# Message loop of a graph kernel: the index tiles of the gathers are filled by transfers of the sync engine in place of GpSimd copies

## The chip, the cores and the metric

One core of a Trainium2 chip runs the whole kernel in one launch. The metric is the device time of that core in microseconds, median over the runs. Engines are PE (TensorE), DVE (VectorE), ACT (ScalarE), POOL (GpSimd) and SP (SyncE). In this kernel SP only issues DMAs, and POOL issues the gathers.

## What is computed

The reference puts four graph layers behind one another on 625 nodes of 512 values: a mean aggregation, a transformer over the edges, a weighted graph convolution, and a message layer over 20,000 edges. The change is in the last:

```python
def _L3_gnn_ref(x, edge_index, edge_attr, W1, b1, W2, b2, W3, b3, W4, b4, gamma, beta):
    src, dst = (edge_index[0], edge_index[1])
    edge_feat = jnp.concatenate([x[src], x[dst], edge_attr], axis=-1)
    h = mish(edge_feat @ W1 + b1)
    messages = mish(h @ W2 + b2)
    agg = jax.ops.segment_sum(messages, dst, num_segments=x.shape[0])
    u = mish(jnp.concatenate([x, agg], axis=-1) @ W3 + b3)
    out = u @ W4 + b4
    y = x + out
    ...
```

## The kernel before

`edge_layer` is the last of the kernel's stages and takes its second part, from about 877 us on. x @ W1 is not computed per edge: two tables, src_table and dst_table, hold x times the two blocks of W1 for each node, and an edge needs one row of each, added. The edges are sorted by target. A tile is 128 edges, a pair is 2 tiles (PT = 2), a group is 2 pairs, so 512 edges; there are 40 groups (PAIRS = 80 pairs, the last group nearly empty). The loop goes pair by pair: one step per pair, and `run_steps` writes it on every engine, 16 steps ahead of a hardware loop of 4 steps a pass and some steps behind it. `s(n)` and `g(n)` give the step and the group with a lag, `on(n)` says whether the step of n before exists, and `a` is the step modulo 4.

What each engine does in a step:

- POOL: waits until the ring buffer is free (semaphore turned: PE has transposed the pair that was four before, so a count of s-3), and issues two gathers of the first table for pair s (L1661, into ring buffer a of 4). Then it waits for the landing of those of the pair before and issues two gathers of the second table for pair s-1, which add onto the first (L1692). In every even step, from 12 on, it also issues an addition of a finished group's sums to agg in HBM (L1706).
- PE: transposes the gathered rows of a pair (L1762), adds the attributes' product (L1770, L1771), sums an older pair by its one-hot tile (L1795), and multiplies by W2 in three parts, 24 matmuls (L222).
- ACT and DVE: the two Mish functions, each a chain that goes between them. The first: ACT L1887, DVE L1977, ACT L1893, L1895, L1897, DVE L2020, then DVE splits the result in two parts (L2029, L2031) for PE. The second: DVE L2003, ACT L1903, DVE L2023, ACT L1906, L1909, L1890, DVE L1984. In even steps DVE also makes the one-hot tile (L1994), takes the sums (L2017) and splits the attributes (L2040, L2042).
- SP: loads the attributes of a group (L1621) into one of two slots when the split of the group before in that slot is done (attr_low).

The row numbers that a gather reads lie in an index tile: `index[0]` and `index[1]`, each of 128 x 2 x 2 x 2 int32 (4 KB), hold the numbers of one group, source and target. All numbers lie in SBUF in `pair_index` from the start of the stage on. In an even step, POOL waits for turned, then for the landing of the second-table gathers of pair s-3, which are the last readers of the tile (dst_added), and then copies 128 x 8 numbers out of `pair_index` (`copy_index`, L1655). It waits for its own copy (index_ready, L1656) and goes on with the gathers. `settle` is an increment of a semaphore that nobody waits for; the waits ahead of it in POOL's sequencer are carried by it (L163 in the profile).

Of the kernel before, what the change touches and what calls it, by code (L numbers as in the profile page):

```python
# [159 lines left out]
def settle(k, eng):  # L160


    eng.sem_inc(k.settled, 1)  # L163
# [1302 lines left out]
def edge_layer(nc, k):  # L1466

    PT = 2
    EDGE = PT * P
    RING = 4  # L1470
    LATE = 4
    OWN = [(m, f) for m in range(KF) for f in range(2)]
    ctx = ExitStack()
    with ctx:
        sb, pb, sem = scope(ctx, nc, "edge")
# [7 lines left out]
        pair_index = sb("pair_index", [P, TILES // PT, 2, PT], I32)  # L1483
        index = [sb(f"index{a}", [P, 2, 2, PT], I32) for a in range(2)]
# [28 lines left out]
        ps_sum = [pb(f"sump{a}", [P, D]) for a in range(2)]  # L1513
        S = {n: sem(n) for n in (
            "loaded_once", "index_made", "vec", "sca", "made", "w1_split", "zeroed", "var_ready", "rstd_ready", "h_ready",
            "index_ready", "turned", "z1_made", "attr_high", "attr_low",
            "e1_ready", "u1_ready", "inner1_ready", "q1_ready", "h1_ready", "hi_ready", "lo_ready",
            "z2_made", "z2_ready", "e2_ready", "u2_ready", "square2_ready", "log2_ready", "q2_ready", "h2_ready",
            "onehot_ready", "pair_summed", "sum_taken", "mish_vec", "mish_sca", "u_ready",
# [5 lines left out]
        from_loaded = [sem(f"from_loaded{a}") for a in range(RING)]  # L1525
        dst_added = [sem(f"dst_added{a}") for a in range(RING)]
        attr_loaded = [sem(f"attr_loaded{a}") for a in range(2)]
        PAIRS = GROUPS * TPG // PT
        DEPTH = 16
        low, high = slice(0, EATTR), slice(EATTR, P)  # L1530
# [49 lines left out]
        with nc.Block() as block:  # L1580
            @block.sync
            def _(sp):
                sp.dma_start(b1[:, :], k.dram["b1"][None, :].to_broadcast([P, D])).then_inc(loaded["b1"], 16)
                for part in (low, high):
                    sp.dma_start(w1_raw[part, :], k.dram["w1"][2 * D:2 * D + EATTR, :]).then_inc(S["loaded_once"], 16)
                sp.dma_start(w2, k.dram["w2"].rearrange("(c p) n -> p c n", p=P)).then_inc(loaded["w2"], 16)
                sp.dma_start(b2, k.dram["b2"][None, :].to_broadcast([P, D])).then_inc(S["loaded_once"], 16)
                halves = k.dram["w3"].rearrange("(c p) n -> p c n", p=P)
                sp.dma_start(w3[0], halves[:, 0:KF, :]).then_inc(loaded["w3"], 16)
                sp.dma_start(b3[:, :], k.dram["b3_cols"]).then_inc(loaded["b3"], 16)  # L1590
                rows_used = LAST_EDGES // TPG
                for n, name in enumerate(("src_tiles", "dst_mark")):
                    for t in range(TPG):
                        tile = (GROUPS - 1) * TPG + t
                        sp.dma_start(last_raw[t * rows_used:(t + 1) * rows_used, n:n + 1],
                                     k.dram[name][0:rows_used, tile:tile + 1],
                                     allow_slow_non_contiguous=True).then_inc(S["last_loaded"], 16)
                sp.wait_ge(S["zeroed"], 1)
                for i in range(NT):
                    sp.dma_start(k.agg[i * P:(i + 1) * P, :], zero).then_inc(zero_stored, 16)  # L1600
                sp.dma_start(k.agg[NP:NP + WIN, :], zero[0:WIN]).then_inc(zero_stored, 16)
                for name, table, stored in (("src", k.src_table, src_stored), ("dst", k.dst_table, dst_stored)):
                    for i in range(NT):
                        tab.need(sp, (name, i))
                        sp.dma_start(table[i * P:(i + 1) * P, :], tables[name][:, i, :]).then_inc(stored, 16)

                last_attr = k.dram["attr_T"][:, (GROUPS - 1) * GROUP:GROUPS * GROUP].rearrange(
                    "f (t p) -> f t p", t=TPG)[:, :, 0:LAST_EDGES // TPG]

                def step(s, g, a, on, is_late):  # L1610
                    if a % 2 == 0 and on(0):

                        slot, o = a // 2, g(0) % GROUPS
                        if on(4):

                            sp.wait_ge(S["attr_low"], g(2))
                        for part in (low, high):
                            if is_late and is_late(0) == LATE:
                                sp.dma_start(attr[slot][part, 0:LAST_EDGES], last_attr).then_inc(attr_loaded[slot], 16)
                            else:  # L1620
                                sp.dma_start(attr[slot][part, :], k.dram["attr_T"][:, bass.ds(o * GROUP, GROUP)]  # L1621
                                             ).then_inc(attr_loaded[slot], 16)

                n = run_steps(sp, step)

                for name in ("b4", "gamma", "beta"):
                    sp.dma_start(rows[name], k.dram[name][None, :].to_broadcast([P, D])).then_inc(loaded["rows"], 16)
                tab.need(sp, ("own",) + OWN[-1])
                sp.dma_start(w3[1], halves[:, KF:2 * KF, :]).then_inc(loaded["w3b_w4"], 16)
                sp.dma_start(w4, k.dram["w4"].rearrange("(c p) n -> p c n", p=P)).then_inc(loaded["w3b_w4"], 16)  # L1630

                sp.wait_ge(sum_stored, (n * GROUPS + (GROUPS - LATE)) * 16)

                sp.wait_ge(S["turned"], n * PAIRS + (PAIRS - 1))
                for i in range(NT):
                    sp.dma_start(agg[:, i, :].bitcast(F32), k.agg[i * P:(i + 1) * P, :]).then_inc(agg_loaded[i], 16)
                for i in range(NT):
                    sp.wait_ge(S["x_ready"], i + 1)
                    sp.dma_start(k.dram["out"][i * P:(i + 1) * P, :], k.x[:, i, :]).then_inc(out_stored, 16)
                sp.wait_ge(out_stored, 16 * NT)  # L1640

            @block.gpsimd
            def _(pool):
# [1 line left out]
                pool.wait_ge(S["made"], 1)  # L1645
                pool.memset(attr_w_rest[high, :].bitcast(F32), 0.0).then_inc(S["made"], 1)
                pool.wait_ge(S["made"], 2)
                pool.wait_ge(S["index_made"], 2)

                def copy_index(s, g, a, last=False):  # L1650
                    if last:
                        pool.wait_ge(S["last_ready"], 2)
                    settle(k, pool)
                    pair = last_index[:, :, :, :] if last else pair_index[:, bass.ds(s(0) % PAIRS, 2), :, :]
                    pool.tensor_copy(index[a // 2][:, :, :, :], pair).then_inc(S["index_ready"], 1)  # L1655
                    pool.wait_ge(S["index_ready"], g(-2))  # L1656
                    settle(k, pool)

                def gather_src(a):
                    for j in range(PT):  # L1660
# [2 lines left out]
                            in_offset=bass.IndirectOffsetOnAxis(ap=index[a // 2][:, a % 2, 0, j:j + 1], axis=0)  # L1663
                        ).then_inc(from_loaded[a], 16)

                for a in (0, 2):
                    copy_index(lambda add: a + add, lambda lag: (a - lag) // 2, a)
                pool.wait_ge(src_stored, 16 * NT)
                settle(k, pool)
                for a in range(RING):  # L1670
# [5 lines left out]
                def step(s, g, a, on, is_late):  # L1676
                    if on(0) and on(4):

                        pool.wait_ge(S["turned"], s(-3))
                        settle(k, pool)  # L1680
                        if a % 2 == 0:

                            pool.wait_ge(dst_added[(a - 3) % RING], s(-3) // RING * (16 * PT) + 16 * PT)
                            copy_index(s, g, a, is_late and is_late(0) == LATE)
                        gather_src(a)
                    if on(1):

                        ring = (a - 1) % RING
                        pool.wait_ge(from_loaded[ring], s(-1) // RING * (16 * PT) + 16 * PT)
                        settle(k, pool)  # L1690
                        for j in range(PT):
                            pool.indirect_dma_start(  # L1692
                                out=from_rows[ring][:, j, :].bitcast(F32), out_offset=None, in_=k.dst_table,
                                in_offset=bass.IndirectOffsetOnAxis(ap=index[ring // 2][:, ring % 2, 1, j:j + 1], axis=0),
                                compute_op=ALU.add).then_inc(dst_added[ring], 16)

                    if a % 2 == 0 and on(14) and not (is_late and is_late(14)):

                        pool.wait_ge(sum_stored, g(14) * 16 + 16)
                    if a % 2 == 0 and on(12) and not (is_late and is_late(12)):  # L1700

                        slot = a // 2
                        start = pool.value_load(k.starts[0:1, bass.ds(g(12), 1)], min_val=0, max_val=NP)
                        pool.wait_ge(S["sum_taken"], g(10))
                        settle(k, pool)
                        pool.dma_start(k.agg[bass.ds(start, WIN), :].rearrange("n (s c) -> s n c", s=2),  # L1706
                                       sum_rows[slot][:, :], accum_op=ALU.add).then_inc(sum_stored, 16)
# [511 lines left out]
```

## Time and profile before

| | |
|---|---|
| median of 3 runs | 1679.72 us (1679.65 to 1692.11) |
| the profiled execution's own time | 1672.88 us |
| its span in the profile | 1671.0 us, mean granted clock 0.987 |
| busy share of the span | PE 94%, DVE 71%, ACT 66%, POOL 41% |
| steady part of the message loop | about 1000 to 1560 us, 17.15 us a group |
| additions to agg issued by POOL | 36 |

The profile is one execution. A timeline row gives the start, the duration, the engine, the line of the program, the operation and its tiles, the count of instructions merged into the row, and in brackets the idle time of the engine before it with what ended it. "issue" there means that the profile shows nothing it waited for. A row of a DMA on POOL shows the time in which POOL writes its descriptors, not the transfer. A row of POOL's sequencer has the engine name POOLq, one of SP's SPq. Spans on POOL are rough.

### The profile page before, as it was taken

What the parts mean: (1) busy time and instruction counts of PE and PEld (TensorE: products, weight loads), DVE (VectorE), ACT (ScalarE), POOL (GpSimd) and SP (SyncE); (2) the same over time, 40 slices, a digit from 0 to 9 for tenths busy, and PEclk for the clock granted to TensorE, in tenths of its full rate; (3) what the DMA queues carried; (4) which work ended last, traced back from release to release, by engine and by line L of the source; (5) the groups of instructions that cost most, each with busy time, mean ns of one, the idle gap of its engine ahead of it and who ended that gap; (6) DMA issues with size and microseconds to landing.
All of it is one profiled execution on the core that took longest, in us unless ns stands there. A gap on an engine that the chain in (4) does not pass through costs nothing. (4 is left out here: it accounts for less than half of the span.)

```text
span 1671.0 us, 25082 instructions
## 1 busy us (share of the span) xinstructions
PE 1566.8 (94%) x8530; PEld 1218.3 (73%) x8530; DVE 1190.2 (71%) x1900; ACT 1097.2 (66%) x1531; POOL 686.0 (41%) x495
## 2 busy tenths in 40 slices
PE   5789699999999999999999999999999999999987
PEld 4765486878687868877854777777777777777774
DVE  8867546564655546565733588989989898998967
ACT  9841536554554455444530699999999999999962
POOL 3410120110012001200302788888888888888500
PEclk9999799999999999999999999999999999999989
DMA  3001140013002200211107767677777777777710
GB/s 104 0 19 65 39 133 25 1 51 113 26 20 67 85 21 32 62 52 63 53 1 228 156 139 150 145 144 148 138 152 144 148 145 142 151 135 155 162 38 31
DMA packets 107046, 153.94 MB, mean 92 GB/s; under 512 B 42042, under 2 KB 47034, under 8 KB 106466
## 3 DMA queue, kind: packets, MB, share of 16 engines
q0 software_dynamic: 72832, 87.84, 27.3%
q1 hardware_dynamic: 34146, 65.21, 12.0%
q8 instruction: 41, 0.67, 0.2%
q14 instruction: 27, 0.22, 0.0%
HBM read 141.02 MB, written 11.73 MB: 91 GB/s over the span
## 5 line engine op out<-in xcount | busy, mean ns | idle before, releaser
L1692 POOL DMA_INDIRECT edge_gathered<-dst_table,edge_index x158 | 257.3, 1629 | 57.4 <-issue 53.9
L222 PE MATMUL edge_z2p<-edge_w_hi,edge_h_hi 128*128 128x512 f32 x628 | 255.3, 407 | 6.8 <-issue 3.5
L1661 POOL DMA_INDIRECT edge_gathered<-src_table,edge_index x158 | 221.5, 1402 | 85.3 <-issue 33.6
L222 PE MATMUL edge_z2p<-edge_w_hi,edge_h_lo 128*128 128x512 f32 x628 | 248.5, 396 | 0.0
L222 PE MATMUL edge_z2p<-edge_w_lo,edge_h_hi 128*128 128x512 f32 x628 | 248.3, 395 | 0.0
L904 POOL TENSOR_TENSOR tr_cw<-w_c,tr_cw 32x1024 fp32r<-32x1024 f32 x8 | 19.0, 2373 | 367.5 <-ACT tr_cw L1118 367.5
L915 POOL TENSOR_TENSOR h<-h,tr_row_b 128x512 f32<-128x512 f32 x40 | 61.1, 1562 | 263.9 <-ACT C L1160 263.6
L222 PEld LDWEIGHTS edge_z2p<-edge_w_hi,edge_h_hi 128*128 128x128 f32 x628 | 117.9, 188 | 61.3 <-issue 36.3
L2020 DVE SCALAR_TENSOR_TENSOR edge_early<-edge_early,edge_z1p 128x1024 f32<-128x1024 f32 x79 | 96.5, 1221 | 59.8 <-ACT edge_early L1897 44.0
L222 PEld LDWEIGHTS edge_z2p<-edge_w_hi,edge_h_lo 128*128 128x128 f32 x628 | 118.0, 188 | 28.5
L222 PEld LDWEIGHTS edge_z2p<-edge_w_lo,edge_h_hi 128*128 128x128 f32 x628 | 118.1, 188 | 24.9
L931 PE MATMUL tr_one<-tr_yT_hi,tr_w_hi 128*128 128x256 f32 (+1 forms) x384 | 118.5, 309 | 5.0 <-issue 4.4
L931 PE MATMUL tr_one<-tr_yT_hi,tr_w_lo 128*128 128x256 f32 (+1 forms) x384 | 117.5, 306 | 0.0
L931 PE MATMUL tr_one<-tr_yT_lo,tr_w_hi 128*128 128x256 f32 (+1 forms) x384 | 117.5, 306 | 0.0
L1893 ACT ACTIVATE edge_early<-edge_early 128x1024 f32<-128x1024 f32 x79 | 83.5, 1056 | 48.8 <-DVE edge_early L1977 46.4
L1017 PE MATMUL tr_two<-tr_kT,tr_qT 128*128 128x320 f32 x320 | 101.7, 444 | 1.4 <-ACT C L1211 1.3
L1205 ACT ACTIVATE hT<-hT,tr_nmax 128x640 f32<-128x640 f32 x56 | 46.3, 827 | 83.7 <-DVE tr_nmax L1368 82.5
L2003 DVE TENSOR_TENSOR edge_late<-edge_z2p,w_c 128x1024 f32<-128x1024 f32 x79 | 96.5, 1222 | 4.9 <-PE edge_z2p L222 1.1
L2031 DVE TENSOR_TENSOR edge_h_lo<-edge_early,edge_h_hi 128x1024 fp32r<-128x1024 f32 x79 | 96.9, 1226 | 2.7
L1984 DVE SCALAR_TENSOR_TENSOR edge_late<-edge_late 128x1024 f32<-128x1024 f32 x79 | 95.8, 1213 | 0.3 <-ACT edge_late L1906 0.3
L1895 ACT ACTIVATE edge_early<-edge_early 128x1024 f32<-128x1024 f32 x79 | 83.7, 1060 | 2.5
L1897 ACT ACTIVATE edge_early<-edge_early 128x1024 f32<-128x1024 f32 x79 | 83.6, 1058 | 2.5
(356 smaller groups left out, 3985.8 us busy)
## 6 DMA issues: line engine op xcount, KB each, us to landing
w_c<-in_attr_T SPq DMA_DIRECT2D x78, 128.0 KB
agg<-edge_sum_rows POOLq DMA_DIRECT2D x36, 128.0 KB
w_a<-in_wv SPq DMA_DIRECT2D x4, 1024.0 KB, 5.3
w_b<-in_wq SPq DMA_DIRECT2D x4, 1024.0 KB, 5.4
w_a<-in_wk SPq DMA_DIRECT2D x4, 1024.0 KB, 7.7
w_b<-in_wo SPq DMA_DIRECT2D x4, 1024.0 KB, 7.0
w_a<-in_m SPq DMA_DIRECT2D x4, 1024.0 KB, 5.4
w_b<-in_m SPq DMA_DIRECT2D x4, 1024.0 KB, 5.3
```

What stands on the lines that cost most here:

```text
L222: mm = pe.matmul(out, a, b, start=(n == 0), stop=(n == last))
L931: mm = pe.matmul(out, a, b, start=(start and n == 0), stop=(stop and n == len(terms) - 1))
L1017: mm = pe.matmul(bank[:, f, 0:HALF], qT[:, h, i * P:(i + 1) * P], kT[:, h, f * HALF:(f + 1) * HALF], start=True, stop=True)
L1661: pool.indirect_dma_start(out=from_rows[a][:, j, :].bitcast(F32), out_offset=None, in_=k.src_table, in_offset=bass.IndirectOffsetOnAxis(ap ...
L1692: pool.indirect_dma_start(out=from_rows[ring][:, j, :].bitcast(F32), out_offset=None, in_=k.dst_table, in_offset=bass.IndirectOffsetOnAxis ...
L1893: act.activation(m1[one], m1[one], ACT.Square).then_inc(S["inner1_ready"], 1)
L1895: act.activation(m1[one], m1[one], ACT.Ln, bias=1.0).then_inc(S["inner1_ready"], 1)
L1897: act.activation(m1[one], m1[one], ACT.Exp, scale=-1.0).then_inc(S["q1_ready"], 1)
L1984: dve.scalar_tensor_tensor(h2[new], m2[new], 0.5, z2[new], ALU.subtract, ALU.mult).then_inc(S["h2_ready"], 1)
L2003: dve.tensor_tensor(cols(z2[two], D), cols(ps_z2[:, :], D), b2[:, None, :].to_broadcast([P, PT, D]), ALU.add).then_inc(S["z2_ready"], 1)
L2020: dve.scalar_tensor_tensor(m1[one], m1[one], 0.5, ps_z1[one][:, :], ALU.subtract, ALU.mult).then_inc(S["h1_ready"], 1)
L2031: dve.tensor_tensor(h1_lo[one][:, :, :], cols(m1[one], EDGE), h1_hi[one][:, :, :].bitcast(F32), ALU.subtract).then_inc(S["lo_ready"], 1)
```

## The change

The copy on POOL goes. SP fills the index tiles by a DMA from `pair_index` to `index[slot]`, both in SBUF. POOL signals that a tile is free (index_free) at the end of the odd step before the one that needs it, after it has waited there for the landing of the second-table gathers of pair s-2 (which is pair s-3 as seen from the even step). In the even step POOL waits for the DMA's landing (index_loaded) instead of copying. In SP's order the wait for index_free and the new DMA stand ahead of the attribute loads of the same step; the first two fills stand ahead of the table stores. The last group's tile comes from `last_index`, by the same DMA.

```diff
+        index_loaded = [sem(f"index_loaded{a}") for a in range(2)]
...
                 sp.dma_start(k.agg[NP:NP + WIN, :], zero[0:WIN]).then_inc(zero_stored, 16)
+                sp.wait_ge(S["index_made"], 2)
+                for slot in range(2):
+                    sp.dma_start(index[slot][:, :, :, :], pair_index[:, 2 * slot:2 * slot + 2, :, :]).then_inc(index_loaded[slot], 16)
...
                         if on(4):
-
+                            at = s(0) % PAIRS
+
+                            sp.wait_ge(S["index_free"], g(2))
+                            if is_late and is_late(0) == LATE:
+                                sp.wait_ge(S["last_ready"], 2)
+                                pair = last_index[:, :, :, :].rearrange("p a b c -> p (a b c)")
+                            else:
+                                pair = pair_index[:, :, :, :].rearrange("p a b c -> p (a b c)")[:, bass.ds(at * (2 * PT), 4 * PT)]
+                            sp.dma_start(index[slot][:, :, :, :].rearrange("p a b c -> p (a b c)"), pair).then_inc(index_loaded[slot], 16)
                             sp.wait_ge(S["attr_low"], g(2))
...
-                pool.wait_ge(S["index_made"], 2)
-
-                def copy_index(s, g, a, last=False):
-                    if last:
-                        pool.wait_ge(S["last_ready"], 2)
-                    settle(k, pool)
-                    pair = last_index[:, :, :, :] if last else pair_index[:, bass.ds(s(0) % PAIRS, 2), :, :]
-                    pool.tensor_copy(index[a // 2][:, :, :, :], pair).then_inc(S["index_ready"], 1)
-                    pool.wait_ge(S["index_ready"], g(-2))
-                    settle(k, pool)
...
-                for a in (0, 2):
-                    copy_index(lambda add: a + add, lambda lag: (a - lag) // 2, a)
+                for slot in range(2):
+                    pool.wait_ge(index_loaded[slot], 16)
...
                         if a % 2 == 0:
-
-                            pool.wait_ge(dst_added[(a - 3) % RING], s(-3) // RING * (16 * PT) + 16 * PT)
-                            copy_index(s, g, a, is_late and is_late(0) == LATE)
+                            pool.wait_ge(index_loaded[a // 2], g(0) // 2 * 16 + 16)
+                            settle(k, pool)
                         gather_src(a)
...
+                    if a % 2 == 1 and on(-1) and on(3):
+
+                        pool.wait_ge(dst_added[(a - 2) % RING], s(-2) // RING * (16 * PT) + 16 * PT)
+                        pool.sem_inc(S["index_free"], 1)
```

How it moves instructions on POOL, in the hardware loop, from the odd step to the even step behind it. Before (edge_index is the index tile, edge_gathered the ring, ISA and REGISTER_ALU are the sequencer's):

```order
L1661 DMA edge_gathered<-src_table,edge_index 128x512 [waits edge_turned]
L1661 DMA edge_gathered<-src_table,edge_index 128x512
L1689 ISA
L1692 DMA edge_gathered<-dst_table,edge_index 128x512 [waits edge_from_loaded0]
L1692 DMA edge_gathered<-dst_table,edge_index 128x512
L1655 ISA [waits edge_turned,edge_dst_added3]
L1655 COPY edge_index<-edge_pair_index 128x8
L1656 REGISTER_ALU
L1661 DMA edge_gathered<-src_table,edge_index 128x512 [waits edge_index_ready]
```

The same place after the change:

```order
L1663 DMA edge_gathered<-src_table,edge_index 128x512 [waits edge_turned]
L1663 DMA edge_gathered<-src_table,edge_index 128x512
L1690 ISA
L1693 DMA edge_gathered<-dst_table,edge_index 128x512 [waits edge_from_loaded0]
L1693 DMA edge_gathered<-dst_table,edge_index 128x512
L1684 ISA [waits edge_dst_added3,edge_turned]
L1663 DMA edge_gathered<-src_table,edge_index 128x512 [waits edge_index_loaded1]
```

The copy and the wait for it are gone, and the wait for the landing (dst_added) now stands ahead of the one for turned, with the increment of index_free between them, which is no row here. SP's queue in the hardware loop before, two steps:

```order
L1621 ISA [waits edge_attr_low]
L1621 DMA w_c<-in_attr_T 64x512 x2
L1621 ISA [waits edge_attr_low]
L1621 DMA w_c<-in_attr_T 64x512 x2
L1569 ISA
```

and after the change:

```order
L1627 ISA [waits edge_index_free]
L1627 DMA edge_index<-edge_pair_index 128x8
L1633 ISA [waits edge_attr_low]
L1633 DMA w_c<-in_attr_T 64x512 x2
L1627 ISA [waits edge_index_free]
L1627 DMA edge_index<-edge_pair_index 128x8
L1633 ISA [waits edge_attr_low]
L1633 DMA w_c<-in_attr_T 64x512 x2
```

Each pair of attribute loads now has the index transfer and its wait ahead of it. PE, ACT and DVE keep their order.

## Rows read from the trace of the kernel before

**Rows 1.** Waits, message loop (920 to 1630): who waited for whom: us, times, longest.
```profile
ACT edge_early L1893 <- DVE edge_early L1977: 46.4, 39, 3.1
DVE edge_early L2020 <- ACT edge_early L1897: 44.0, 52, 3.3
...
POOL edge_gathered L1661 <- POOL edge_index L1655: 30.6, 38, 0.8
...
PE edge_z1p L1762 <- DMA edge_gathered<-dst_table,edge_index: 1.6, 1, 1.6
```

**Rows 2.** Timeline of ACT, one group: start, duration, instruction, idle before.
```profile
1313.15 1.06 ACT L1893 ACTIVATE edge_early<-edge_early 128x1024 f32<-128x1024 f32 x1 [1.14 <-DVE edge_early L1977]
...
1323.28 1.06 ACT L1897 ACTIVATE edge_early<-edge_early 128x1024 f32<-128x1024 f32 x1
...
1330.32 1.06 ACT L1893 ACTIVATE edge_early<-edge_early 128x1024 f32<-128x1024 f32 x1 [1.17 <-DVE edge_early L1977]
```

**Rows 3.** Timeline of DVE, the same group.
```profile
1317.57 0.69 DVE L2023 TENSOR_SCALAR edge_late<-edge_late 128x1024 f32<-128x1024 f32 x1
...
1324.37 1.22 DVE L2020 SCALAR_TENSOR_TENSOR edge_early<-edge_early,edge_z1p 128x1024 f32<-128x1024 f32 x1 [0.45 <-issue]
...
1326.11 0.70 DVE L2029 CAST edge_h_hi<-edge_early 128x1024 fp32r<-128x1024 f32 x1
...
1327.99 0.65 DVE L2040 CAST edge_attr_parts<-w_c 128x512 fp32r<-128x512 f32 x1
...
1329.45 0.84 DVE L1977 TENSOR_SCALAR edge_early<-edge_early 128x1024 f32<-128x1024 f32 x1
```

**Rows 4.** Timeline of PE, transposes of three pairs in the same group.
```profile
1312.73 0.81 PE L1762 MATMUL edge_z1p<-edge_ident_r,edge_gathered 128*128 128x128 f32 x8
...
1321.39 0.80 PE L1762 MATMUL edge_z1p<-edge_ident_r,edge_gathered 128*128 128x128 f32 x8
...
1329.86 0.80 PE L1762 MATMUL edge_z1p<-edge_ident_r,edge_gathered 128*128 128x128 f32 x8
```

**Rows 5.** Line L163 on POOL's sequencer, 1313.4 to 1313.8: ns, first and last start.
```profile
L163 POOLq EVENT_SEMAPHORE  x2: 17/17/17, 1313.6 to 1313.7; - x2
```

**Rows 6.** Timeline of POOL, the same group.
```profile
1316.17 1.56 POOL L1692 DMA_INDIRECT edge_gathered<-dst_table,edge_index  x1 [0.30 <-issue]
1317.16 1.12 POOL L1655 COPY edge_index<-edge_pair_index 128x8 int32 x1
1319.08 2.03 POOL L1661 DMA_INDIRECT edge_gathered<-src_table,edge_index  x1 [0.80 <-POOL edge_index L1655]
...
1325.14 1.75 POOL L1692 DMA_INDIRECT edge_gathered<-dst_table,edge_index  x1 [0.30 <-issue]
1326.31 2.08 POOL L1706 DMA_DIRECT2D agg<-edge_sum_rows  x1
1328.69 1.08 POOL L1661 DMA_INDIRECT edge_gathered<-src_table,edge_index  x1 [0.30 <-issue]
```

**Rows 7.** Timeline of POOL, start of the loop: last gather of pair 1, first copy.
```profile
923.59 1.53 POOL L1692 DMA_INDIRECT edge_gathered<-dst_table,edge_index  x1 [0.30 <-issue]
...
929.25 0.34 POOL L1655 COPY edge_index<-edge_pair_index 128x8 int32<-128x8 int32 x1 [0.46 <-DMA edge_gathered<-dst_table,edge_index]
```

**Rows 8.** SP: its waits from 880 to 1630, and its attribute issues near 1312.5 (ns).
```profile
SPq L1621 <- DVE edge_attr_parts L2042: 556.3, 37, 16.0
...
L1621 SPq DMA_DIRECT2D w_c<-in_attr_T x2: 475/648/822, 1312.5 to 1313.0; - x2
```

**Rows 9.** DMA issues from 920 to 1630: count, size, median us to landing.
```profile
edge_gathered<-agg SPq DMA_DIRECT2D x5, 256.0 KB, 4.1
```

**Rows 10.** Timeline of DVE, before the first addition to agg.
```profile
985.42 0.42 DVE L2040 CAST edge_attr_parts<-w_c 128x512 fp32r<-128x512 f32 x1
...
986.59 0.69 DVE L1977 TENSOR_SCALAR edge_early<-edge_early 128x1024 f32<-128x1024 f32 x1
```

**Rows 11.** Timeline of DVE, end of the loop, beside an addition to agg.
```profile
1583.14 0.98 DVE L2029 CAST edge_h_hi<-edge_early 128x1024 fp32r<-128x1024 f32 x1
```

More of the change, by code:

```diff
@@ L1515, in edge_layer @@
             "loaded_once", "index_made", "vec", "sca", "made", "w1_split", "zeroed", "var_ready", "rstd_ready", "h_ready",
-            "index_ready", "turned", "z1_made", "attr_high", "attr_low",
+            "turned", "index_free", "z1_made", "attr_high", "attr_low",
             "e1_ready", "u1_ready", "inner1_ready", "q1_ready", "h1_ready", "hi_ready", "lo_ready",
```

## Prediction

> **What bounds the kernel now.** I read the waits of the message loop first, then a timeline of one group (two steps) on each engine, then the same instructions at another phase of the loop. The table of waits says who is late: ACT waits for DVE (46.4 us, 39 times), DVE for ACT (44.0 us, 52 times), and PE waited for a gather once in its loop stretch, 1.6 us [rows 1]. The longest wait that the change touches is POOL's own, 30.6 us in 38 waits for its copy [rows 1]: it belongs to an engine that nobody waits for.
>
> The timelines show why. From ACT's first instruction of a group, 1313.15, to its end at 1323.28 + 1.06 = 1324.34, ACT runs without a gap; at 1324.37 DVE's product L2020 starts, which waited for it, and DVE runs without a gap to the end of L1977, 1329.45 + 0.84 = 1330.29; at 1330.32 ACT's L1893 starts, which waited for that [rows 2, 3]. Start to start is 1330.32 - 1313.15 = 17.17 us: this ring of ACT and DVE is the group's period. PE is close behind: its transposes start at 1312.73, 1321.39 and 1329.86, so one step takes 8.66 us and the other 8.47 [rows 4]. The shorter is PE without a wait, so PE alone would need 2 x 8.47 = 16.94 us. The period can fall by 17.15 - 16.94 = about 0.2 us a group and no more, whatever happens on POOL.
>
> POOL looks full in its timeline, since every gather starts 0.3 us after the one before, but it has time to spare. The wait for the transposes that free the ring buffer (turned) is passed at 1313.6, in POOL's sequencer [rows 5], while the copy behind it runs only at 1317.16, after the two gathers already queued [rows 6]. That wait belongs to step s, and it asks for pair s-4, whose transposes ran at 1312.73. Pair s-3 is then transposed at 1321.39, s-2 at 1329.86, s-1 at 1338.5. The second-table gather of pair s-1 is issued until 1325.14 + 1.75 = 1326.89 [rows 6]. At the start of the loop a landing shows: issued until 923.59 + 1.53 = 925.12, landed when the copy was released at 929.25, 4.1 us later [rows 7]. So pair s-1 is there at 1331.0 and PE is 7.5 us from missing it.
>
> **The change, part by part.**
>
> *Removed: POOL's copy and its two waits.* The copy takes 1.12 us, of which 1317.73 - 1317.16 = 0.57 lie beside the gather before it (1316.17 + 1.56), and 0.80 of idle follows [rows 6]: 1.12 - 0.57 + 0.80 = 1.35 us a group, 1319.08 - 1317.73 as a check, and 40 groups make 54 us of POOL. Its cover is the 7.5 us of slack, so the end moves by 0. If the cover were gone these 54 us would be the gain, and nothing in the rows says it is.
>
> *Added on POOL:* the landing wait for pair s-3 moves from the start of the even step to the end of the odd one, with the increment of index_free; behind it in the queue stand only the wait for turned and the gathers of step s. It was passed at 1313.7 at the latest [rows 5], so POOL loses nothing by it.
>
> *Added on SP:* one issue a group, priced by its neighbours at 0.48 to 0.82 us [rows 8], and a wait in front of it that holds back the attribute loads of the same step. SP idles 556.3 us in 37 waits, 15 us a group [rows 8], and the split that reads them (L2040) comes for that slot two groups later, at 1327.99 + 17.15. Cost 0.
>
> *Added wait: index_loaded.* Signal at 1313.7, issue 0.5 to 0.8, landing between nothing and the 4.1 us of the nearest row, a 256 KB load [rows 9]: the tile is there between 1314.2 and 1318.6. POOL could start at 1317.73 + 0.30 = 1318.03. So the gathers of step s start at 1318.0 to 1318.9 in place of 1319.08; I take 1318.0, as 4 KB is the smaller end. POOL gains 1 us at first and up to 5 over the groups, until turned or the index stops it. All of it is slack.
> The Trainium skill (DMA: Bandwidth & Descriptors, Anatomy of one DMA) gives a fixed cost of some 2 us to a DMA from GpSimd, most of it completion; an estimate by it would put the tile at 1316.5, before POOL is free. It speaks against the exchange where the ring is short (the copy takes 0.34 us when POOL is idle [rows 7]); no run so far shows the cost for a small transfer of SP.
>
> *Start.* At step 4 POOL is not ahead: the copy starts at the landing, 929.25, takes 0.34, and the same 0.80 of idle follows: the gather comes 1.14 us later [rows 6, 7]. Now it is signal, issue and landing, 0.5 to 4.9 us: the gather comes between 0.6 us earlier and 3.8 us later, once. PE holds several ready pairs there. I take +1 us. The two first fills stand on SP before the table stores, which wait for DVE; 0.
>
> *Moved: POOL against DVE.* This is the term with a sign. In the ring of ACT and DVE stand two instructions that take longer than they need: L2040 0.65 and L1977 0.84 [rows 3]. Nineteen groups earlier, before the additions to agg began, they took 0.42 and 0.69 [rows 10]. The difference, 0.23 + 0.15 = 0.38 us, is in every group of the ring. Beside them POOL issues the addition to agg (ends 1326.31 + 2.08 = 1328.39) and a gather (ends 1328.69 + 1.08 = 1329.77) [rows 6]; L2040 ends 0.25 after the one and L1977 0.52 after the other, as if each had been let go then. With POOL 1 us or more earlier the addition ends near 1327.0 to 1327.4, before L2040 asks at 1327.99. Bounds: all 0.38 goes, but PE caps the gain at 0.2; or the same POOL work hits L2023 and L2029 of the ring. I take -0.1 us in the 33 to 36 groups with an addition: -3.5 us.
> The Trainium skill (SBUF — State Buffer, Who interferes with whom) states that DVE in its two-port mode and GpSimd share a port pair as an exclusive lock. The stretched rows agree with it. By it, taking any GpSimd copy away should also free DVE; the rows say that this copy stretches nothing: L2023 at 1317.57 takes 0.69 with the copy beside it at 1317.16, so that gain is 0.
>
> *Sum.* The profiled execution took 1672.88 us (span 1671.0): +1 - 3.5 = 1670.4. The median of the runs, 1679.72, is 6.84 above it; there the forecast is 1677.5.
>
> **Rivals.**
>
> *A, POOL's new place hits DVE harder (slower).* Mechanism: the addition and the gathers, now earlier, fall on L2023 and L2029, which stand in the ring (L2029 at 1326.11 with 0.70, L2023 right before it) [rows 3] and are not stretched today. Price: one such hit is shown at the end of the loop, L2029 0.98 us in place of 0.69, beside an addition [rows 11]. Two hits make +0.58 a group; if the 0.38 of today stays too, 36 x 0.58 = +21, 1700 us. It decides from 0.47 a group on (1% over 36 groups). Against it: POOL's addition already lies on L2029 today (from 1326.31) without stretching it.
>
> *B, the stretch goes altogether.* The ring falls to 17.15 - 0.38 = 16.8, PE holds at 16.94: 36 x 0.2 = -7, 1672.5 us. For it: a shift of 1 us suffices for L2040. Against: the gather behind the addition moves too and may stretch the next.
>
> *C, the new transfer is late.* PE waits once it lands more than 7.5 us after it should; each us beyond that costs up to 1 us a group, 2 us would be 1750. Nothing near it: 256 KB land in 4.1.
>
> *D, POOL doesn't come forward at all,* since the index lands at 1318.6 to 1319: nothing changes but the start, 1680.5.
>
> **How the numbers follow.** Forecast 0.50, A 0.14, B 0.20, C 0.03, D 0.13. The forecast's own range is 1672 to 1685. The runs of before differ among themselves by 0.4% (profiled against median) and more, so the low end is B less that, 1666; the high end takes in most of A, 1694. About 1% is what a measurement of this kernel can tell from no change, 16.8 us. Faster by that is closed by PE's 16.94 (0.2 x 36 = 7 us): 0.04, for an error in that floor. Slower by it are C and most of A: 0.14. Within: 0.82.
>
> **What would show it.** Right: POOL's waits for its copy are gone, POOL shows some idle time before the even step's gather or runs it near 1318.0 of the same phase, PE still waits for no gather, the group's period is 16.94 to 17.15, and L2040 falls towards 0.42. For A, L2023 or L2029 above 0.69 in most groups and a period above 17.5. For B, a period of 16.94 and PE without any wait for L2003. For C, PE waiting for second-table gathers in the loop. The prediction is wrong if the period moves by more than 0.2 downward, since then PE's floor was misread, or if ACT and DVE keep their ring and the time still rises.

## The result, and the profile after

The changed kernel takes 1716.36 us (median of 4 runs, 1710.29 to 1726.27), the kernel before 1680.4 beside it: ratio 1.020, 95% interval 1.0136 to 1.027. It is slower (the whole interval lies above 1; whether it is slower by 2% it leaves open), where I forecast 1677.5 and no change. The profiled execution took 1718.4 us, its span is 1716.5, which is 45.5 more than the 1671.0 of before.

The waits of the message loop after the change (920 to 1630; who waited for whom: us, times, longest):

```profile
POOL edge_gathered L1663 <- DMA edge_index<-edge_pair_index: 88.7, 33, 5.6
DVE edge_sum_rows L2022 <- DMA agg<-edge_sum_rows: 55.2, 27, 3.6
...
ACT edge_late L1914 <- DVE edge_late L2028: 45.0, 38, 3.2
DVE edge_early L2025 <- ACT edge_early L1902: 41.7, 43, 3.3
...
ACT edge_early L1898 <- DVE edge_early L1982: 32.7, 37, 3.1
...
PEld edge_z1p L1767 <- DMA edge_gathered<-dst_table,edge_index: 22.4, 19, 2.4
```

Against [rows 1] three waits are new or grown. POOL waits for the index transfer, 88.7 us in 33 groups, 2.7 each. DVE waits 27 times until an addition to agg has landed and the sums' buffer is free (55.2 us). PE's weight loads wait 19 times for gathered rows (22.4 us; PE itself waited once in the loop before). DVE and PE, which in the loop before waited for what POOL issues once at most, now do so in 19 and more groups: POOL has come onto the path.

POOL's timeline, one group after the change (start, duration, instruction, idle before; it answers [rows 6]):

```profile
1313.81 1.77 POOL L1663 DMA_INDIRECT edge_gathered<-src_table,edge_index  x1 [3.77 <-DMA edge_index<-edge_pair_index]
1315.89 1.45 POOL L1663 DMA_INDIRECT edge_gathered<-src_table,edge_index  x1 [0.30 <-issue]
1317.64 1.57 POOL L1693 DMA_INDIRECT edge_gathered<-dst_table,edge_index  x1 [0.30 <-issue]
1319.52 1.56 POOL L1693 DMA_INDIRECT edge_gathered<-dst_table,edge_index  x1 [0.30 <-issue]
1320.50 2.56 POOL L1711 DMA_DIRECT2D agg<-edge_sum_rows  x1
...
1328.81 1.56 POOL L1693 DMA_INDIRECT edge_gathered<-dst_table,edge_index  x1 [0.30 <-issue]
1332.44 1.19 POOL L1663 DMA_INDIRECT edge_gathered<-src_table,edge_index  x1 [2.07 <-DMA edge_index<-edge_pair_index]
```

SP's timeline in the same group, and below it pieces of the chain that ended last (start, duration, what), with the transfers of the group before and of the group after:

```profile
1324.27 0.52 SPq L1627 DMA_DIRECT2D edge_index<-edge_pair_index  x1
1325.04 1.12 SPq L1633 DMA_DIRECT2D w_c<-in_attr_T  x2
```

```profile
1305.25 0.10 SPq L1627
1305.36 0.05 issue
1305.41 7.61 DMA edge_index<-edge_pair_index
1313.06 0.75 issue
1313.81 0.33 POOL edge_gathered L1663
...
1343.57 6.38 DMA edge_index<-edge_pair_index
```

Read together they give a ring that closes once a group. POOL issues the four gathers of the even step, 1313.81 to 1319.52 + 1.56 = 1321.08: 7.27 us. The second-table gathers among them are the ones whose landing frees the tile, and SP issues the next transfer at 1324.27: 3.19 us. POOL goes on at 1332.44, 8.17 us after that issue began (7.4 of transfer, if POOL's restart takes the 0.75 seen in the chain; 7.61 and 6.38 are the transfers of the groups on either side). The sum is 7.27 + 3.19 + 8.17 = 18.63 us, and of the engines that run the program only POOL and SP have a part in it. The parts follow one another without slack: by the trace's semaphore updates the second-table gathers have landed at 1324.04, 0.23 before SP's issue, and the transfer at 1331.64, 0.80 before POOL goes on. POOL's other work of the group, the addition and the odd step's four gathers until 1330.37, lies beside it and ends 2.07 us early. Over 1100 to 1560 POOL's additions start on average 18.56 us apart (23 groups), before 17.15 (26). From the first addition to the last it is 637.3 us (1002.8 to 1640.1) in place of 592.9 (1000.5 to 1593.4): 44.4 of the 45.5 us that the span is longer.

How the lateness reaches DVE and PE, in their timelines of the same stretch ([rows 3, 4] before):

```profile
1314.63 0.42 DVE L2045 CAST edge_attr_parts<-w_c 128x512 fp32r<-128x512 f32 x1
...
1315.80 0.69 DVE L1982 TENSOR_SCALAR edge_early<-edge_early 128x1024 f32<-128x1024 f32 x1
...
1320.94 0.93 DVE L2028 TENSOR_SCALAR edge_late<-edge_late 128x1024 f32<-128x1024 f32 x1
1321.79 0.96 DVE L2034 CAST edge_h_hi<-edge_early 128x1024 fp32r<-128x1024 f32 x1
...
1330.60 0.42 DVE L2022 TENSOR_SCALAR edge_sum_rows<-edge_sump 128x256 f32<-128x256 f32 x1 [3.21 <-DMA agg<-edge_sum_rows]
```

```profile
1335.41 0.88 PE L1767 MATMUL edge_z1p<-edge_ident_r,edge_gathered 128*128 128x128 f32 x8 [2.00 <-DMA edge_gathered<-dst_table,edge_index]
```

DVE sat 3.21 us for an addition that POOL had issued until 1323.06, and PE 2.00 us for gathered rows. The two instructions that I watched fell as I said: from 1100 to 1560 L2045 takes 0.42 to 0.46 in all 25 groups and L1982 0.69 or 0.70 in all 50 steps. Two others stretch in about half of the groups: L2028 to 0.84 or more in 14 of 49 steps, L2034 to 0.83 or more in 13 of 49. SP's idle time is now one wait per group for the signal (532.0 us in 34 waits, in place of the 556.3 for attr_low of [rows 8]):

```profile
SPq L1627 <- POOLq L1700: 532.0, 34, 18.6
```

One thing more stands in the traces: the transfer isn't slow from the start. These are its rows in the variant with four index tiles (its section is below), where no engine waits for it: the count of issues, the size and the median us from issue to landing, first for 925 to 995, then for 1000 to 1560.

```profile
edge_index<-edge_pair_index SPq DMA_DIRECT2D x5, 4.0 KB, 2.8
edge_index<-edge_pair_index SPq DMA_DIRECT2D x30, 4.0 KB, 7.0
```

Between the two stretches POOL issues its first addition to agg, at 997.12. The gathers run in both, and the DMA share is 0.78 in the first and 0.76 in the second, so the gathers' load by itself doesn't make the 7 us. In the changed kernel POOL waits for a tile once at the start (5.16 us, until 937.85) and next at 1014.4, after its first addition at 1002.76. This points to the additions, which come once a group; no run takes them out, so it isn't shown.

### The profile page after: what moved, and what is told of

Read it like the earlier page. It is cut to its first block and busy times, and to the rows that moved or that the text cites. A ratio compares the mean times of both kernels' runs of the same rounds, so it can differ in the third digit from the quotient of the medians.

```text
span 1716.5 us, 25064 instructions
## 1 busy us (share of the span) xinstructions
PE 1581.7 (92%) x8530; PEld 1224.5 (71%) x8530; DVE 1186.7 (69%) x1900; ACT 1098.0 (64%) x1531; POOL 668.9 (39%) x455
## 3 DMA queue, kind: packets, MB, share of 16 engines
q1 hardware_dynamic: 39906, 65.38, 11.9%
## 5 line engine op out<-in xcount | busy, mean ns | idle before, releaser
L1693 POOL DMA_INDIRECT edge_gathered<-dst_table,edge_index x158 | 288.5, 1826 | 55.6 <-issue 49.8
L1663 POOL DMA_INDIRECT edge_gathered<-src_table,edge_index x158 | 193.6, 1225 | 150.6 <-DMA edge_index<-edge_pair_index 88.7
L1914 ACT ACTIVATE edge_late<-edge_late 128x1024 f32<-128x1024 f32 x79 | 84.0, 1063 | 51.2 <-DVE edge_late L2028 45.0
L1898 ACT ACTIVATE edge_early<-edge_early 128x1024 f32<-128x1024 f32 x79 | 83.3, 1055 | 36.2 <-DVE edge_early L1982 33.4
L1800 PE MATMUL edge_sump<-edge_late,edge_onehot 128*64 128x256 f32 x576 | 79.5, 398 | 13.2 <-DVE edge_late L1989 9.8
```

Of the source, the lines that this page charges most:

```text
L1663: pool.indirect_dma_start(out=from_rows[a][:, j, :].bitcast(F32), out_offset=None, in_=k.src_table, in_offset=bass.IndirectOffsetOnAxis(ap ...
L1693: pool.indirect_dma_start(out=from_rows[ring][:, j, :].bitcast(F32), out_offset=None, in_=k.dst_table, in_offset=bass.IndirectOffsetOnAxis ...
L1800: mm = pe.matmul(ps_sum[slot][side * WIN:(side + 1) * WIN, 0:D // 2], onehot[slot][:, b * PT + j, :], h2[b][:, j * D + side * (D // 2):j * ...
L1898: act.activation(m1[one], m1[one], ACT.Square).then_inc(S["inner1_ready"], 1)
L1914: act.activation(m2[two], m2[two], ACT.Square).then_inc(S["square2_ready"], 1)
```

## Experiments

Eleven runs; the kernel before ran beside each and took 1679.9 to 1681.7 us. Theory R is the ring above. P stands for two theories: in the expectations that don't say what it is, POOL's changed place against DVE; where they speak of POOL's issuing, its issue time plus its idle time. T, L, O and X are told where they are used.

### What of the change costs nothing

**The transfers without the wait.** The kernel before with the same transfers into tiles that nobody reads, the signals, and SP's wait.

```diff
+    spare = [sb(f"spare{a}", [P, 2, 2, PT], I32) for a in range(2)]
...   SP, ahead of the attribute loads
+    sp.wait_ge(S["index_free"], g(2))
+    sp.wait_ge(spare_loaded[slot], ...)     # the transfer before into this tile
+    sp.dma_start(spare[slot]..., pair).then_inc(spare_loaded[slot], 16)
...   POOL, end of the odd step
+    pool.wait_ge(dst_added[(a - 2) % RING], ...)
+    pool.sem_inc(S["index_free"], 1)
```

> The kernel before, with its copies, plus all that the change adds beside POOL's wait for the landing: the index_free signal at the end of the odd step, SP's wait for it, and the same 37 transfers of 4 KB, into spare tiles that nobody reads. Theory R (the ring tile free - transfer - gathers - landing - tile free, once a group, is longer than the group): no engine waits for these transfers, so within 5 us of the kernel before, 1675 to 1687. Theory T (the 5,640 small packets, or SP's holding back of the attributes, slow the gathers): at least half of the loss, 1698 or more. Theory P (POOL's changed place against DVE costs it): as before, since POOL's order of busy instructions is kept.

Measured: 1677.63 us, ratio 0.9975 (0.9943 to 1.0008). The small packets (144 a transfer, 5,328 in this run), SP's wait ahead of the attributes and the signal cost nothing that shows.

**The moved wait.** The kernel before with only the wait for dst_added moved to the end of the odd step.

```diff
-    pool.wait_ge(dst_added[(a - 3) % RING], ...)     # even step, ahead of the copy
+    pool.wait_ge(dst_added[(a - 2) % RING], ...)     # end of the odd step
+    settle(k, pool)
```

> The kernel before, with only the wait for the landing of pair s-3 moved from the even step to the end of the odd one, where the change has it; the copy stays. All theories but one expect no change, 1675 to 1687: the wait was passed before the one for turned that follows it. If the moved wait itself held POOL's queue, it would show 1690 or more.

Measured: 1677.77 us, ratio 0.9986 (0.9951 to 1.0021).

### The wait alone

The kernel of the first experiment with one wait more. Nothing reads the spare tile, so the wait is all that is added.

```diff
+    pool.wait_ge(spare_loaded[a // 2], g(0) // 2 * 16)     # even step
     copy_index(s, g, a, ...)
```

> The kernel of the first run (the kernel before with the transfers into spare tiles, the signals and SP's wait: no change in time) with one thing more: POOL waits in the even step for the landing of the spare tile ahead of its copy. Nothing reads that tile. Theory R (the ring free signal, transfer, gathers, landing, which in the changed kernel is 18.6 us): the ring closes by this wait alone, and the copy behind it adds 0.3 to 0.5: 1715 to 1755 us. Theory L (traffic, SP's order, the copy's removal or the gathers' new place, but not the wait): as the first run, 1672 to 1686.

Measured: 1728.75 us, ratio 1.031 (1.0252 to 1.0364). The waits of its loop, two rows of POOL's timeline a group apart, and the transfer in its chain:

```profile
DVE edge_sum_rows L2032 <- DMA agg<-edge_sum_rows: 67.3, 30, 3.4
POOL edge_index L1663 <- DMA edge_spare<-edge_pair_index: 60.7, 31, 3.8
...
PEld edge_z1p L1777 <- DMA edge_gathered<-dst_table,edge_index: 33.2, 29, 2.3
```

```profile
1317.02 0.19 POOL L1663 COPY edge_index<-edge_pair_index 128x8 int32 x1 [1.10 <-DMA edge_spare<-edge_pair_index]
...
1336.05 0.19 POOL L1663 COPY edge_index<-edge_pair_index 128x8 int32 x1 [2.70 <-DMA edge_spare<-edge_pair_index]
```

```profile
1328.40 7.34 DMA edge_spare<-edge_pair_index
```

The same three waits, a transfer of 7.34 us, 19.03 us from copy to copy in this group and 18.90 us a group on average. From 1677.6 to 1728.8 by a wait alone: the added wait index_loaded is the part of the change that costs, and what it closes is the ring. That the loss is larger than the change's fits the copy, which stays here and stands in the ring: 18.90 - 18.56 = 0.34 us a group, 12 us in 36 groups, and the medians differ by 12.4.

### Opening the ring

Four index tiles in place of two, filled two groups ahead on the same signal; the loop is written 8 steps a pass for it. The second run below is the control with the 8 steps and two tiles. The version with four tiles also puts three start-up loads on one semaphore, ahead of the loop, which the control doesn't have.

```diff
-    index = [sb(f"index{a}", [P, 2, 2, PT], I32) for a in range(2)]
+    index = [sb(f"index{a}", [P, 2, 2, PT], I32) for a in range(4)]
...
-    at = s(0) % PAIRS
+    at, to = s(4) % PAIRS, (phase[0] // 2 + 2) % 4
...
-    sp.dma_start(index[slot]..., pair).then_inc(index_loaded[slot], 16)
+    sp.dma_start(index[to]..., pair).then_inc(index_loaded[to], 16)
```

> The changed kernel with four index tiles in place of two, each filled two groups ahead on the same signal, so that POOL's wait for the transfer stays but the transfer has a whole group more. Written for a theory that the earlier runs suggest and that replaces mine: POOL's own issuing is what counts. In the traces of the kernel before, of the change, of the eight copies and of the other order, the eight gathers and the addition of a group take POOL 15.9 to 16.3 us with their 0.3 us gaps, and the rest of the group is POOL's idle time (1.0, 2.3, 3.8 and 2.2 us), so every idle us of POOL is a us of the group. Theory P (POOL's issue time plus its idle time): the wait of some 2.3 us goes, POOL needs 16.3 us and the group falls back to 16.9 to 17.2, where PE or ACT and DVE hold it: 1672 to 1684 us. Theory L (the traffic or SP's order, not POOL's wait): no change, 1710 to 1725. Theory R (ring over the tile as long as the group, my first account): as P.

> Control for the four tiles: the changed kernel with only the hardware loop written eight steps a pass in place of four, still two index tiles. All theories: no change against the changed kernel, 1708 to 1725 us. Should it come out under 1700, the gain of four tiles is not the tiles' alone.

Measured: four tiles 1673.65 us, ratio 0.996 (0.9917 to 1.0002); the control 1718.97 us, ratio 1.022 (1.011 to 1.033). The four tiles again, run more often:

> The kernel with four index tiles again, in more rounds, for its size against the kernel before. Its group was 16.92 us in the first trace, where the kernel before has 17.15, and PE without a wait 16.94: 0.23 x 36 groups = 8 us less, ratio 0.995. Same (no gain in the end): ratio 0.999 or above.

Measured: 1672.15 us, ratio 0.9958 (0.993 to 0.9986). This is the one version whose interval lies below 1, by 0.4%. Busy time of each engine from 1000 to 1560, in the order PE, PEld, DVE, ACT, POOL, then granted clock, DMA share and GB/s; of the kernel before, of the change, and of the four tiles (the first run):

```profile
1000.00:1560.00 560.00, 554.79 (x3133) 435.53 (x3133) 503.95 (x588) 517.86 (x523) 464.07 (x328) 1.00 0.73 146
```

```profile
1000.00:1560.00 560.00, 528.83 (x2947) 409.55 (x2947) 467.30 (x553) 485.47 (x490) 416.82 (x272) 0.99 0.67 135
```

```profile
1000.00:1560.00 560.00, 560.00 (x3178) 441.19 (x3175) 503.06 (x597) 526.08 (x531) 415.42 (x297) 1.00 0.76 150
```

The transfers still take 7.0 us (median, rows above), and the loss is gone. With four tiles PE is busy in all 560 us, and the group takes 16.92 us, the 16.94 that I had read as PE's floor. POOL, with neither copy nor a late tile, has time to spare that its timeline shows once a group:

```profile
1329.29 0.99 POOL L1667 DMA_INDIRECT edge_gathered<-src_table,edge_index  x1 [2.00 <-issue]
```

### SP's order

The changed kernel with the signal's wait and the transfer behind the attribute loads.

```diff
+    sp.wait_ge(S["attr_low"], g(2))
+    (attribute loads)
     sp.wait_ge(S["index_free"], g(2))
     (index transfer)
-    sp.wait_ge(S["attr_low"], g(2))
-    (attribute loads)
```

> The changed kernel with the wait for index_free and the transfer behind the attribute loads of the same step on SP, in place of ahead of them. Theory L (SP's order costs): better than the change, under 1700 us. Theories P and R: the transfer starts later only when attr_low is later than index_free; 1712 to 1740, not better.

Measured: 1725.77 us, ratio 1.028 (1.017 to 1.038). Not better, so SP's order isn't the cause.

### A longer ring without a transfer

The kernel before with eight, then with four copies per tile, each waiting for the one before.

```diff
+    for n in range(COPIES):
         pool.tensor_copy(index[a // 2][:, :, :, :], pair).then_inc(S["index_ready"], 1)
-    pool.wait_ge(S["index_ready"], g(-2))
+        pool.wait_ge(S["index_ready"], g(0) * COPIES + n + 1)
```

> The kernel before, with the copy of the index tile made 8 times, each waiting for the one before: no transfer is added, only time between the tile's release and its first reader, 7 x about 1.1 us when POOL has nothing queued, near 8 us. Theory R: the same ring is now longer than a group by 1 to 2.5 us, so 39 groups cost 40 to 95 us, 1720 to 1775. Theory T: no small packets, so nothing from that side; the copies alone would take POOL's time, and with the 7.5 us of slack that the prediction counted on PE would not see it: below 1700.

> The kernel before with four dependent copies per tile in place of one. In the run with eight, each further copy took POOL 0.19 + 0.17 us. Theory P: POOL needs 16.1 of issuing and has no idle time but the copy's 1.0 in a group of 17.15, so three further copies lengthen it by 3 x 0.36 = 1.1 us, 38 groups x 1.1 = 41: 1715 to 1727 us. Theory R (a latency ring of some 13 us over the tile, with 4 us to spare): no change, 1674 to 1686. My prediction's slack of 7.5 us as a lasting reserve: no change either.

Measured: eight copies 1789.14 us, ratio 1.064 (1.057 to 1.071); four copies 1686.16 us, ratio 1.0043 (1.0004 to 1.008). Theory P, that POOL's issue time is fixed near 16 us so that every idle us counts, expected 1715 to 1727 for four copies and missed. Theory R's 1674 to 1686 is all but met by the four, while the eight went past the 1775 that I had set as its upper end. The window of the run with four copies (same columns):

```profile
1000.00:1560.00 560.00, 556.92 (x3147) 436.96 (x3147) 502.51 (x591) 520.03 (x525) 448.12 (x423) 1.00 0.75 145
```

POOL is busy for less (448.12, before 464.07) although it makes three copies more per group. Worked out from the timelines of 1100 to 1560, the eight gathers and the addition with their 0.3 us gaps take 14.9 us a group here (period 17.08, of which 2.15 around the copies), 15.1 with four tiles, 16.1 in the kernel before and 16.3 in the changed one. So POOL's time for the same work isn't fixed, 14.9 to 16.3 us a group, and four copies fit in. With eight it is 16.1, and 16.1 + 3.8 around the copies is the 19.8 us of its period; why the issuing doesn't shrink there no run shows. A ring of latencies of some 13 us, as I had put it for four copies, fits their 0.4% but not the 6.4% of eight: there it is POOL's sum in order that counts. Both bounds on POOL exist: its work in order, and the ring. The changed kernel is held by the ring, since POOL idles while it waits for the tile and four tiles cure it.

### The other order: a miss explained

The changed kernel with the second-table gathers of pair s-1 ahead of the waits of the even step.

```diff
     even step:
+    (wait from_loaded, two gathers of the second table for s-1)
     (wait turned, wait index_loaded, two gathers of the first table for s)
-    (wait from_loaded, two gathers of the second table for s-1)
```

> The changed kernel, with POOL's order turned round in the even step: the second-table gathers of pair s-1 are issued ahead of the waits for turned and index_loaded and of the gathers of pair s. The last readers of the tile no longer stand behind a wait for the other tile, so the ring spans two groups (34 us) for the same work. Theory R: the loss goes, 1672 to 1690. Theory T or P: the transfers, packets and instructions are the same, so it stays above 1705.

Measured: 1713.74 us, ratio 1.016 (1.0088 to 1.0238). R's 1672 to 1690 was missed. The wait for the tile is all but gone from its list (0.9 us, once), and another stands in its place (waits of POOL, a row of its timeline, and the chain):

```profile
POOL edge_gathered L1695 <- DMA edge_gathered<-src_table,edge_index: 92.1, 36, 5.2
```

```profile
1333.32 1.70 POOL L1695 DMA_INDIRECT edge_gathered<-dst_table,edge_index  x1 [2.53 <-DMA edge_gathered<-src_table,edge_index]
```

```profile
1324.85 7.70 DMA edge_gathered<-src_table,edge_index
```

The new order puts the second-table gathers of a pair next behind the odd step's gathers that they wait for, and the landing of such a gather takes 7.70 us here. To see whether that alone costs, I put the same order into the kernel before, with its copies and without any transfer:

> The kernel before, copies and all, with only the order of the third run: in the even step the second-table gathers of pair s-1 ahead of the waits and the first-table gathers of pair s. It asks why that order didn't help the changed kernel (1713.74 where theory R expected 1672 to 1690). In that run's trace a first-table gather issued in the odd step from 1323.40 on had landed for POOL only at 1332.57, and nothing was queued in between, so the order seems to make a ring of its own: landing of the odd step's gathers, 0.75, four gathers, an addition and two gathers, 18.1 us a group. Theory O (the order alone costs): slower than before here too, without any transfer, 1695 to 1720 us. Theory X (the transfer was still what held that run, R being wrong): 1672 to 1686 here.

Measured: 1728.76 us, ratio 1.0297 (1.0239 to 1.0355), above the 1720 that I had set as the upper end. Its first wait is

```profile
POOL edge_gathered L1694 <- DMA edge_gathered<-src_table,edge_index: 79.1, 36, 5.4
```

So that experiment opened one ring and closed another of nearly the same length: the group takes 18.13 us in it, 18.43 in the kernel before with the new order, 18.56 in the changed kernel. It says nothing against R, and it couldn't have tested it.

## Why the prediction was wrong

**What bounds the kernel: right.** ACT and DVE hold 17.15 and PE has a floor of 16.94. With four tiles, L2040's counterpart takes 0.45 and L1977's 0.69, and the group takes 16.92 with PE never idle: rival B's mechanism, at B's price.

**Removed copy: right as a price.** 0 as long as others hold the loop. With nothing put in its place but a tile that is there in time, 0.23 a group comes of it, the 0.2 that I had allowed at most.

**Moved wait and SP's issue, 0: right.** The runs with the moved wait alone and with the transfers alone show both.

**Added wait index_loaded: this step failed, in two ways.** First its size: "landing between nothing and the 4.1 us of the nearest row, a 256 KB load", with 4 KB as the smaller end, so tile ready by 1318.6 at the latest. The transfer took 7.61, 7.4 and 6.38 us. A 256 KB row was no upper bound for 4 KB: the time isn't in the bytes. That row's five loads are issued at 1602, after the last gather and the last addition. The trace of the kernel before holds a nearer one, SP's attribute loads in the loop: from 1004 on, their semaphore's last update comes 6.6 to 8.9 us after the first of the two issues. Second its cover: "POOL gains 1 us at first and up to 5 over the groups ... All of it is slack." I held the delay of one gather against the 7.5 us by which a pair is early. But the wait stands in a ring that closes once a group with two tiles: landing of the gathers that free the tile, signal, transfer, the next gathers. In a ring a reserve is used once, and what counts is its length against 17.15. From the after rows: 7.27 + 3.19 + 8.17 = 18.63. With my own bound for the transfer (0.82 + 4.1, and 0.8 for the restart) it would be 7.27 + 3.19 + 5.7 = 16.2, under the period, so the size decided; but I never formed this sum, and so did not see that less than 1 us lay between nothing and a loss in every group.

The Trainium skill (DMA: Bandwidth & Descriptors, Anatomy of one DMA) puts the fixed cost of a DMA issued from GpSimd near 2 us. Here SP's 4 KB between two places in SBUF took 2.8 us (median) beside the gathers alone and 7.0 once the additions had begun, and the measurement decides. The same page of the Trainium skill (SWDGE vs HWDGE vs iDMA) says that DMAs of both kinds run on the same engines, which go round between their queues. A short transfer that lands late agrees with that, but the DMA share, 0.78 and 0.76, doesn't tell the 2.8 from the 7.0.

**Start and POOL against DVE: beside the point.** The stretches moved as forecast (L2040's to 0.42, L1977's to 0.69), but by luck: I had them go because POOL comes earlier, and it comes later. Rival A's stretches appear on L2028 and L2034 in about half of the groups. They aren't the cause: with four tiles the counterpart of L2028 is stretched in every group (27 of 55 steps, 0.80 to 0.89), and the group takes 16.92. L2034's add at most 0.27 in 13 steps, under 4 us from 1100 to 1560, where 25 groups lose 1.41 each, 35 us. The sum has a slip as well: 1670.4 + 6.84 is 1677.2 and not 1677.5, which changes nothing.

**Rival C named the right end by the wrong condition.** "PE waits once it lands more than 7.5 us after it should ... Nothing near it": it needed no such lateness, only a ring longer than the period, and it deserved far more than 0.03. Its sign in the trace, PE waiting for second-table gathers in the loop, is there, behind DVE's wait for the additions, which I hadn't named at all: POOL issues these too.

## What to carry to other kernels

When a copy on an engine becomes a DMA with a wait, draw the ring through the buffer it fills (free signal, transfer, use, landing, free signal) and compare its length with the period of the loop; time by which data is early now is no cover for a wait inside a ring. Price a small DMA from the landings of the same queue in the same stretch of the loop, not from its bytes and not from a stretch with other traffic, and give it a buffer more, so that it is issued a period ahead: two more tiles of 4 KB turned 2% slower into 0.4% faster. And test with the wait alone, on data that nobody reads.

## What the hardware showed that I hadn't expected

A 4 KB transfer from SBUF to SBUF, 144 packets (hardware queue: 34,146 packets before, 39,906 after, for 40 transfers), took 6.4 to 7.6 us in the three groups read from the changed kernel and, in the version with four tiles, 2.8 before the first addition to agg and 7.0 after it (medians), at nearly the same DMA share.

```profile
q1 hardware_dynamic: 39906, 65.38, 11.9%
```

POOL's time for the same gathers isn't a constant. Single ones take 0.96 to 2.59 us from 1100 to 1560 over the traces, and a group's eight with the addition 14.9 to 16.3. The Trainium skill (SBUF — State Buffer, Who interferes with whom) describes a port pair that DVE and GpSimd lock against each other, and the stretched DVE casts beside POOL's issues agree with it; the runs show the spread and not its cause.
